# Identity rows, gathered tiles and counts laid out at pitches of 1280 and 2560 bytes from 256-byte boundaries

## The reference

```python
h = node_states @ kernel
edge_states = h[edges].reshape(edges.shape[0], 2 * units)
scores = leaky_relu(edge_states @ kernel_attention, negative_slope=0.2)[:, 0]
scores_exp = exp(clip(scores, -2.0, 2.0))
tgt = edges[:, 0]
denom = segment_sum(scores_exp, tgt, num_segments=n_nodes)
alpha = scores_exp / (denom[tgt] + EPS)
neigh = h[edges[:, 1]]
out = segment_sum(neigh * alpha[:, None], tgt, num_segments=n_nodes)
# x = layernorm(x + out); then the message network over the same edges, and a second layernorm
```

## Time and profile before

| | us |
|---|---|
| median of 3 runs | 2205.88 |
| lowest, highest | 2204.08, 2208.19 |
| span of the profiled execution | 1891.9 |
| median less that span | 314.0 |
| busy in the span: PE, DVE, ACT, POOL | 1647.0, 1575.9, 1335.9, 1149.9 |

### The profile page before, as it was taken

How to read it: one execution, slowest core, us unless ns; L and a number is a source line. 1 busy time by engine, 2 the same in 40 slices (tenths; PEclk the granted TensorE clock), 3 DMA queues, 4 the chain that set the end, 5 groups by cost and what they waited for, 6 DMA issues and landing times.

```text
span 1891.9 us, 53764 instructions
## 1 busy us (share of the span) xinstructions
PE 1647.0 (87%) x15240; PEld 1425.0 (75%) x15240; DVE 1575.9 (83%) x3400; ACT 1335.9 (71%) x2302; POOL 1149.9 (61%) x1202
## 2 busy tenths in 40 slices
PE   5767888887786776669999999999999999999986
PEld 3445677766575655459999999999999999999964
DVE  5778999887667766769999999999999999999986
ACT  5024678888888873557777777777777777777751
POOL 4212456666665651257777777777777777777720
PEclk9899999998888786979999999999999999999999
DMA  4023467788878871555555554555445555544411
GB/s 100 21 50 71 105 130 144 142 146 148 145 145 137 143 136 34 164 140 142 140 141 140 141 143 140 140 141 141 139 141 142 141 140 142 142 140 141 140 49 34
DMA packets 141999, 236.59 MB, mean 125 GB/s; under 512 B 27997, under 2 KB 92849, under 8 KB 141914
## 3 DMA queue, kind: packets, MB, share of 16 engines
q0 software_dynamic: 49632, 142.89, 31.2%
q1 hardware_dynamic: 92282, 92.71, 21.4%
HBM read 185.78 MB, written 10.66 MB: 104 GB/s over the span
## 4 chain that ended last, share of the span: by engine, by line
PE 55%; DVE 1%; DMA 0%; ACT 0%; issue 0%; POOL 0%; SPq 0%; ACTq 0%; DVEq 0%; POOLq 0%
PE ps L1271 11%; PE ps L1272 10%; PE ps L1277 10%; PE ps L1251 9%; PE psA L1289 6%; PE ps L1246 5%; PE ps L1256 2%; PE ps L990 1%; PE ps L1001 1%; PE ps L998 1%; PE psA L1009 0%; DMA bias_f<-in_L_gnn_bm 0%; DVE x L1062 0%; DMA ga<-table_a,idx 0%; ACT u L1023 0%
## 5 line engine op out<-in xcount | busy, mean ns | idle before, releaser
L1222 POOL DMA_INDIRECT ga<-table_a,idx x784 | 761.4, 971 | 248.0 <-issue 226.4
L615 POOL DMA_INDIRECT head_n<-scr_eye,row_at x250 | 305.1, 1221 | 311.7 <-PE psC L664 209.6
L1271 PE MATMUL ps<-wm_hi,h_hi 128*128 128x256 f32 x1568 | 402.9, 292 | 0.7 <-ACT h_hi L1323 0.7
L1272 PE MATMUL ps<-wm_lo,h_hi 128*128 128x256 f32 x1568 | 381.8, 278 | 0.0
L1327 ACT ACTIVATE h<-ps 128x512 bf16<-128x512 f32 x392 | 234.0, 597 | 177.0 <-PE ps L1277 176.8
L1271 PEld LDWEIGHTS ps<-wm_hi,h_hi 128*128 128x128 f32 x1568 | 294.9, 188 | 30.8 <-ACT h_hi L1323 27.1
L1425 DVE TENSOR_TENSOR h<-rest,h 128x512 bf16<-128x512 f32 x392 | 269.2, 687 | 53.0 <-ACT h L1331 53.0
L1420 DVE SCALAR_TENSOR_TENSOR rest<-ps,h 128x512 f32<-128x512 f32 x392 | 268.0, 687 | 33.2 <-ACT h L1327 16.3
L1272 PEld LDWEIGHTS ps<-wm_lo,h_hi 128*128 128x128 f32 x1568 | 295.5, 188 | 0.0
L673 PE MATMUL psC<-ring_n,ring_m 128*126 x1180 | 235.8, 331 | 56.7 <-DVE ring_n L862 30.1
L1414 DVE SCALAR_TENSOR_TENSOR h_lo<-ps,h_hi 128x512 fp32r<-128x512 f32 x392 | 264.3, 691 | 11.1 <-ACT h_hi L1323 4.6
(11 more groups left out here) (193 smaller groups left out, 2657.6 us busy)
## 6 DMA issues: line engine op xcount, KB each, us to landing
dstb<-scr_dst SPq DMA_DIRECT2D x196, 126.0 KB
cnt<-stage SPq DMA_DIRECT2D x125, 195.3 KB
cnt<-stage SPq DMA_DIRECT2D x125, 109.9 KB
ga<-table_a,idx POOLq DMA_INDIRECT x784, 2.9
bw<-table_b SPq DMA_DIRECT2D x196, 63.0 KB
table_b<-cnt SPq DMA_DIRECT2D x12, 336.0 KB
head_n<-scr_eye,row_at POOLq DMA_INDIRECT x250
table_a<-pr SPq DMA_DIRECT2D x12, 224.0 KB
```

Source lines behind the costliest of these rows:

```text
L615: pool.indirect_dma_start(head_n[:, w % HEADS, s, :], None, scr_eye, bass.IndirectOffsetOnAxis(ap=row_at[:, w % ROWS_AT, s:s + 1], axis=0) ...
L1222: pool.indirect_dma_start(ga[:, u, k, :], None, table_a, bass.IndirectOffsetOnAxis(ap=idx[:, u, k:k + 1], axis=0)).then_inc(gathered[u][k] ...
L1271: pe.matmul(ps2[q][:, t % 2, :], hi, w_hi[:, k, :], start=False, stop=True, skip_group_check=True)
L1272: pe.matmul(ps2[q][:, t % 2, :], hi, w_lo[:, k, :], start=False, stop=True, skip_group_check=True)
```

## The change

The identity matrix gets rows of 640 numbers in SBUF and in HBM (1280 bytes; the additional 14 columns hold the same pattern, so zeros). A slot of `head_n` has 640 numbers, a slot of `stage` 640 float32 numbers (2560 bytes), and `cnt` holds each part of 625 counts at a pitch of 640 (2560 bytes), so a node's row is no longer one contiguous stretch. `cnt`, `head_n` and `stage` are allocated at multiples of 256 bytes. The gather moves whole rows, now 1280 bytes. The stores move the same 625 numbers per piece as before, from and to the new places. `weigh` reads `cnt` with two dims (3 x 625 and 2 x 625) in place of one of 1875 and 1250. The views of `cnt` that serve as staging later start at the second half of `cnt` as before, which now begins 12800 bytes in. No instruction, wait or buffer slot is added or taken away.

```diff
+SWP = 640
+CUT_S = 3
...
-        ones_n = sb("ones_n", [BLK, SW + 1], bf16)
-        eye = sb("eye", [BLK, SBLK, SW + 1], bf16)
+        ones_n = sb("ones_n", [BLK, SWP], bf16)
+        eye = sb("eye", [BLK, SBLK, SWP], bf16)
...
-                                   pattern=[[-1, SW + 1]], channel_multiplier=1).then_inc(eye_ready, 1)
+                                   pattern=[[-1, SWP]], channel_multiplier=1).then_inc(eye_ready, 1)
...
-        def sb(name, shape, dt):
-            return ctx.enter_context(nc.sbuf_tensor(name, shape, dt))
+        def sb(name, shape, dt, align=32):
+            return ctx.enter_context(nc.sbuf_tensor(name, shape, dt, align_bytes=align))
...
-        cnt = sb("cnt", [P, 2, N], fp32)
+        cnt = sb("cnt", [P, 2, SBLK * SWP], fp32, 256)
...
-        head_n = sb("head_n", [P, HEADS, GATHERED, SWE], bf16)
+        head_n = sb("head_n", [P, HEADS, GATHERED, SWP], bf16, 256)
...
-        stage = sb("stage", [P, STAGES, SWE], fp32)
+        stage = sb("stage", [P, STAGES, SWP], fp32, 256)
...
+        counts = cnt[:, :, :].rearrange("p s (k n) -> p s k n", k=SBLK)
...
-                    sp.dma_start(cnt[u * WIN:u * WIN + ROWS_A, (v + 1) % 2, :], stage[0:ROWS_A * SBLK, w % STAGES, 0:SW]).then_inc(stage_out[w % STAGES], 16)
-                    sp.dma_start(cnt[u * WIN + ROWS_A:(u + 1) * WIN, (v + 1) % 2, :], stage[ROWS_A * SBLK:WM, w % STAGES, 0:SW]).then_inc(stage_out[w % STAGES], 16)
+                    sp.dma_start(counts[u * WIN:u * WIN + ROWS_A, (v + 1) % 2, :, 0:SW], stage[0:ROWS_A * SBLK, w % STAGES, 0:SW]).then_inc(stage_out[w % STAGES], 16)
+                    sp.dma_start(counts[u * WIN + ROWS_A:(u + 1) * WIN, (v + 1) % 2, :, 0:SW], stage[ROWS_A * SBLK:WM, w % STAGES, 0:SW]).then_inc(stage_out[w % STAGES], 16)
...
-                    act.activation(stage[0:WME, w % STAGES, :].rearrange("p (k n) -> p k n", k=2), psC[w % 2][0:WME, :, 0:HALF], ACT.Copy,
+                    act.activation(stage[0:WME, w % STAGES, 0:SWE].rearrange("p (k n) -> p k n", k=2), psC[w % 2][0:WME, :, 0:HALF], ACT.Copy,
...
-                slot = pr[:, (v + 1) % PR, slice(*PROB_CUTS[part])]
+                ks = (slice(0, CUT_S), slice(CUT_S, SBLK))[part]
+                slot = pr[:, (v + 1) % PR, slice(*PROB_CUTS[part])].rearrange("p (k n) -> p k n", n=SW)
...
-                dve.tensor_tensor(slot, slot, cnt[0:BLK, v % 2, slice(*PROB_CUTS[part])], ALU.mult).then_inc(prob_ready, 1)
+                dve.tensor_tensor(slot, slot, counts[0:BLK, v % 2, ks, 0:SW], ALU.mult).then_inc(prob_ready, 1)
...
-    scr_eye = dram("scr_eye", (SW, SW + 1), bf16)
+    scr_eye = dram("scr_eye", (SW, SWP), bf16)
```

## The result

| | before | after |
|---|---|---|
| median of 12 runs each, us | 2205.55 | 2197.33 |
| lowest and highest | 2197.66, 2213.53 | 2189.37, 2206.14 |

The ratio is 0.996, with a 95% interval of 0.9944 to 0.9976: 8 us faster, where 28 were forecast. One slow run of the kernel before, 3881 us in the job of the last two experiments, is left out of their ratios.

The account below looks back on a forecast made before the run. It took the DMA engines or their latency to bound attention from 400 to 700 us, sharing with DVE and ACT from 300. Gains of 25.5 + 3 = 28.5 us, plus 314.0 us beside the span, gave 2177 us, range 2158 to 2210.

Parts of the forecast that it names:

- Where the time is: Attention: DMA sets the pace from 400 to 700 us, shares it from 300; no gain before 300; message part unchanged.
- The price of aligned transfers: Gathers and stores: quiet DMA work per window falls 7 to 18%, middle 12% taken, loaded prices assumed to shrink alike.
- my lower bound of 117: Stores: an aligned 2500-byte piece costs at least 117 ns, at most 142, against 160 quiet before.
- rival 1: Gathers and stores: alignment saves only 7% of DMA work, 17 us from 400 to 700 us, 2189 us; chance 0.22.
- my line: Aligned transfers: 25.2 bytes per ns above a fixed part, drawn from rows of 512 and 1024 bytes.
- From DMA work to time: Windows from 4.48 to 4.10 us at 400 to 700 us, 25.5 us gained; 4.35 to 4.22 before, 3 us.
- two limits that close do not overlap perfectly: Windows from 400 to 700 us: DMA gives 3.94 us, ACT 3.96, so 4.10 taken.
- What is late next: From 400 to 700 us: ACT limits next, 3.86 us per window with its waits, 3.96 at 95.7% busy.
- The costs taken as zero: Longer identity making 0.08 us, hidden; `cnt` in two dims 0 to 1.5 us, hidden; tables' stores gain 0 to 2 us.
- Rival 2: Gathers and stores: loaded price comes from two streams meeting, whatever the addresses; nothing gained, 2206 us; chance 0.10.
- Rival 3: Gathers: nothing gained and longer rows paid, 1.1% more DMA work, 4.5 us slower, 2210.4 us; chance 0.11.
- Rival 4: Windows from 300 us: alignment removes the load factor too, ACT alone is left, 39 plus 7 us gained, 2160; chance 0.12.

Follow-up runs that it names:

- the last two experiments: Kernel before with stores cut at column 313, and changed kernel with stores cut at 512: ratios to before 0.9894 and 0.9897.
- second pair: Kernel before and changed kernel, both unchanged, profiled again: spans 1898.0 and 1880.0 us; the changed kernel's ratio there 0.9955.
- hbm_1284: Changed kernel with identity rows of 1284 bytes in HBM, unaligned there, gathered into aligned SBUF slots of 1536 bytes: ratio to before 0.9998.
- thin_both: Kernel before with gathers of 512 bytes per row and stores of 1024 per piece, missing counts cleared once by POOL at the start: ratio 0.9903.
- thin_short: Kernel before with gathers of 512 bytes, stores of 1024, POOL's clears, and ACT's exponential over 1250 of 3125 columns: ratio 0.9864, 1866.3 us.
- rows_1284: Kernel before with identity rows of 1284 bytes at unaligned starts, stores as before: ratio 0.9999.
- split_stores: Changed kernel with each store cut in two by columns, pieces of 1280 and 1220 bytes: ratio to before 0.9853, 1866.3 us.

## Why the prediction was wrong, point by point

**Where the time is: right in place.** Nothing changed before 300 us, and after that the windows came faster and the waits for DMA shorter. The message part kept its time, and the first part too.

**The price of aligned transfers: mis-sized, and the main error.** By the steps of the prediction, on the rows above: gathers 0.433 x 1600 = 693 us for 7.79 MB / 1280 = 6086 rows, 114 ns (103 forecast, 117 before); stores 0.367 x 1600 = 587 us for 2884 pieces, 204 ns (192 forecast, 218 before). A window has (256 x 114 + 125 x 204) / 16 = 3.41 us of DMA work in place of 3.58, 5% less and not 12%. The second pair of traces gives 5% as well, all of it in the stores: 116 ns per row in both, 206 per piece in place of 228.

The step that failed is the one that took the quiet means, 74 ns per row and 160 per piece, for what a row and a piece cost by themselves, and laid the distance to the rows of 512 and 1024 bytes to alignment. Of the 96 pieces behind the earlier trace rows, 41 took at most 110 ns and the longest 385; the shortest take 99 ns before and after the change, which is below my lower bound of 117. Thus 160 was mostly pieces that hold each other up, and aligning them took the quiet median from 162 only to 146. A quiet gather packet did not get cheaper at all (median from 40 to 90 us 193 ns before, 196 after, for 2.2% more bytes). The quiet row of 74 ns had said so, and I noted it for rival 1 and still took the middle.

The Trainium skill ("DMA: Bandwidth & Descriptors", How a descriptor splits into AXI transactions) had given an estimate of 6% by its rule that a transfer is cut at 256-byte boundaries. The total agrees with it better than with my line: 5% measured. The parts do not: the beats give 8% for a gathered row and 4% for a piece, and measured were 0 to 3% and 6 to 10% under load. The shortest packets, where the rule expects a saving too, show none (99 ns both ways; 191 before and 194 after). So that the total comes near may be luck.

The prediction's reading of the earlier trace rows, that only transfers that write SBUF can have a penalty, was not tested, as all the transfers changed here write SBUF. But their other end counts as well, by what the interval of hbm_1284 allows: its SBUF ends are aligned, the rows that it reads from HBM are not, and it shows no gain (0.9998).

**From DMA work to time: too steep.** The forecast took 28.5 us for 12%, 2.4 us per 1%. At that rate 5% would be 12 us; 8 were measured. thin_both shows the reason: with 70% of the DMA work gone, the gain is 18 us, an estimated 25 without the clears. I set the floor at 4.10 us per window and called it the forecast; 4.06 is what a window takes with hardly any transfers. The step "two limits that close do not overlap perfectly" gave the right floor and was wrong about when it is reached. It took ACT for what sets the floor, and thin_short has nearly the same window time with ACT at 84%, so the right value is in part luck.

**What is late next: ACT, only in part.** ACT is busiest there (92% in thin_both), as forecast, but taking 1.6 us per block from it gave 8 us alone and 6 with thin transfers, where 39 would follow if ACT alone set the pace.

**The costs taken as zero: right.** The product with `cnt` in two dims takes 1782 ns on average, as in the earlier trace rows; the identity's making takes 719 ns in place of 708; ACT's wait for the tables' stores went from 11.8 to 9.0 us (13.2 to 8.8 in the second pair).

```profile
L843 DVE TENSOR_TENSOR pr<-pr,cnt 125x1875 f32<-125x1875 f32 (+1 forms) x28 | 49.9, 1782 | 70.8 <-DMA cnt<-stage 33.1 <-ACT pr L744 23.6 <-issue 14.1
...
L191 POOL TENSOR_SCALAR_AFFINE_SELECT eye<-ones_n x5: 718/719/719, 2.0 to 4.7; 125x640 bf16<-125x640 bf16 x5
```

**The rivals.** Rival 1 (a small saving) came nearest: 7% less DMA work where 5% was measured, but 17 us for it where 8 were. Rival 2 is refuted by the changed kernel's own interval and by the quiet stores: addresses do matter. It was half right, for loaded packets are mostly packets that meet others, and alignment changes little of that. Rival 3's extra bytes were not seen (rows_1284). Rival 4, the load factor going away, did not come from alignment; it came from short pieces, as split_stores shows (gather packets 336 ns in place of 443).

## What to carry to other kernels

Align both ends of a transfer to 256 bytes or don't expect it to help: here one end off by 4 bytes left no gain to be seen, and the whole was worth 5% of DMA price under load and 0.4% of time. Before a mean time per piece is taken for its price, look at the shortest packets and at how many come near them: the distance to the mean is waiting, and what shortens a piece does not remove it. Here cutting 2500-byte SBUF-to-SBUF pieces in two was worth three times as much as aligning them. And before a stage is called DMA-bound, measure how much time it loses with the transfers thinned out, and see that what you add for it stays out of the way; a share of 0.8 and 50 us of waits stood for some 25 us.

## What the runs showed of the hardware that was not expected

- A store packet that nothing holds up takes 44 ns for 1024 bytes, 53 for 1280, 81 for 2048 and 99 for 2500, aligned or not. The quiet median is 46, 55, 98, and 146 (aligned) to 162 (unaligned), since of the 2500-byte pieces only a third come near their shortest time and of the 1280-byte pieces two thirds.
- Long pieces also slow other traffic: the gather packet under load takes 443 to 464 ns beside 2500-byte pieces, 336 beside pieces of 1280 and 1220, and 303 beside pieces of 1024. Thinning the gathers left the 2500-byte store at 225 ns. Why was not settled.
- The same program takes 1890 or 2210 us in different jobs, all of it in the message part; in the longer executions PE waits between its matmuls there, and the attention takes the same time.
